# Ten blocks of GpSimd's key parts made in the matrix memory layer instead of the expert layer

## The reference

```
x = x + _L0_xattn_ref(_layernorm(x), ctx_2048, mask)       # one-head attention over the context
x = x + _L0_attn_ref(_layernorm(x), ...)                   # matrix memory (mLSTM), 8 heads, then a gated MLP
x = x + _L0_ffn_ref(_layernorm(x), ...)                    # 16 experts, top 2, and a shared part
x = x + _L1_xattn_ref(_layernorm(x), ctx_2048, ctx_2048)   # 16-head causal attention over the context
```

```
def _rmsnorm(x, w): return w * x * rsqrt(mean(x * x) + 1e-6)
h = _mlstm_parallel(q, k, v, i_pre, f_pre)                 # scores times exp(D - max), by head, causal
h_norm = h * rsqrt(mean(h * h, over the head's 32) + 1e-6) * mh_w
x1 = x + (sigmoid(o_pre) * h_norm) @ w_out
```

## Time and profile before

| | us |
|---|---|
| median of 3 runs | 1100.19 (1099.86 to 1101.62) |
| the profiled execution | 1103.23 |
| its span, first to last instruction | 1101.4 |
| TensorE busy | 1041.8 (95%) |
| VectorE busy | 698.0 (63%) |
| ScalarE busy | 504.3 (46%) |
| GpSimd busy | 234.0 (21%) |

### The profile page before, as it was taken

How to read it: one execution, slowest core, us unless ns; L and a number is a source line. 1 busy time by engine, 2 the same in 40 slices (tenths; PEclk the granted TensorE clock), 3 DMA queues, 4 the chain that set the end, 5 groups by cost and what they waited for, 6 DMA issues and landing times.

```text
span 1101.4 us, 23433 instructions
## 1 busy us (share of the span) xinstructions
PE 1041.8 (95%) x9611; PEld 845.6 (77%) x9611; DVE 698.0 (63%) x1330; ACT 504.3 (46%) x876; POOL 234.0 (21%) x360
## 2 busy tenths in 40 slices
PE   8999999998999989999988899999999999999886
PEld 3765778875777646677775788999999999999764
DVE  3655243247788368888744876776666577677466
ACT  3242232126677448888855624433342233332384
POOL 4701048402132000000010711110001043332120
PEclk9999999999999999999999999999999999999997
DMA  9712346554673517000141000131111122100000
GB/s 383 299 69 79 133 164 214 191 148 121 184 193 106 178 41 263 2 2 2 40 153 40 1 1 20 33 120 41 39 39 58 40 77 68 59 20 10 1 1 10
DMA packets 37158, 100.39 MB, mean 91 GB/s; under 512 B 4033, under 2 KB 12609, under 8 KB 35393
## 3 DMA queue, kind: packets, MB, share of 16 engines
q1 hardware_dynamic: 33152, 87.35, 24.2%
q0 software_dynamic: 2752, 9.44, 2.5%
q10 hardware_dynamic: 1152, 2.16, 0.5%
HBM read 83.73 MB, written 15.20 MB: 90 GB/s over the span
## 4 chain that ended last, share of the span: by engine, by line
PE 81%; DVE 12%; ACT 3%; issue 2%; DMA 1%; POOL 1%; SPq 0%; DVEq 0%; ACTq 0%; POOLq 0%
PE ps L2276 11%; PE ps L2233 10%; PE ps L422 8%; PE ps L1434 6%; PE ps L1790 6%; PE ps L2131 4%; PE ps L2120 4%; PE ps L480 3%; PE ps L1781 3%; PE ps L1582 3%; PE ps L1593 3%; PE ps L415 3%; PE ps L1097 2%; PE ps L1089 2%; PE ps L291 1%
## 5 line engine op out<-in xcount | busy, mean ns | idle before, releaser
L2276 PE MATMUL ps<-vv,prob 128*128 128x129 f32 x1024 | 126.5, 276 | 1.7 <-DVE xn L2463 1.7
L2276 PEld LDWEIGHTS ps<-vv,prob 128*128 128x128 f32 x1024 | 119.6, 191 | 2.5 <-ACT prob L2382 2.1
L2415 DVE TENSOR_REDUCE probT<-ps 128x128 f32<-128x1024 f32 x64 | 82.5, 1290 | 21.9 <-PE ps L2233 12.9
L1716 DVE TENSOR_REDUCE st<-ps 128x1 f32<-128x512 f32 x128 | 82.4, 686 | 18.0 <-PE ps L1582 16.0
L2382 ACT ACTIVATE prob<-prob 128x1024 f32<-128x1024 f32 x64 | 71.1, 1111 | 27.4 <-DVE prob L2427 27.4
L2355 ACT COPY w<-ps 128x128 f32<-128x128 f32 x32 | 8.5, 266 | 160.0 <-PE ps L2242 160.0
L422 PE MATMUL ps<-xT,big 128*128 128x256 f32 x352 | 79.8, 381 | 0.7 <-ACT xT L707 0.7
L2427 DVE TENSOR_TENSOR prob<-ps,probT 128x1024 f32<-128x1024 f32 x64 | 79.6, 1285 | 1.1
L1663 ACT ACTIVATE prob<-ps 128x1024 f32<-128x1024 f32 x64 | 65.8, 1030 | 28.0 <-PE ps L1593 26.8
L422 PEld LDWEIGHTS ps<-xT,big 128*128 128x128 f32 x352 | 66.2, 190 | 11.2 <-ACT xT L707 0.9
L152 POOL TENSOR_SCALAR small<-small 128x4 f32<-128x4 f32 (+1 forms) x44 | 9.9, 226 | 300.3 <-DVE small L2170 156.3
(11 more groups left out here) (476 smaller groups left out, 2282.6 us busy)
## 6 DMA issues: line engine op xcount, KB each, us to landing
big<-blocks_in SPq DMA_DIRECT2D x22, 768.0 KB, 4.3
big<-ctxT_in SPq DMA_DIRECT2D x24, 512.0 KB, 4.1
key_parts<-w POOLq DMA_DIRECT2D x16, 384.0 KB, 4.7
kt<-key_parts SPq DMA_DIRECT2D x32, 192.0 KB, 3.3
vv<-ctx_in SPq DMA_DIRECT2D x2, 2176.0 KB, 24.9
vv<-early_values SPq DMA_DIRECT2D x4, 1088.0 KB, 12.0
kt<-ctxT_in SPq DMA_DIRECT2D x2, 2048.0 KB, 12.4
kt<-key_parts SPq DMA_DIRECT2D x32, 128.0 KB, 3.2
```

What stands on the lines that cost most here:

```text
L1716: dve.tensor_reduce(self.mx[:, u % 2, n:n + 1], k.ps[:, n % 2, :], AX.X, ALU.max).then_inc(s("reduced"), 1)
L2276: last = pe.matmul(k.ps[:, 7, 0:DH + 1], self.prob(u)[:, ch * P:ch * P + P], v, start=(ch == 0), stop=(ch == MC))
L2415: dve.tensor_reduce(self.largest[:, h * P:(h + 1) * P], bank.rearrange("p (c t) -> p t c", t=P), AX.X, ALU.max).then_inc(s("c3_max"), 1)
```

## The change

`Mlstm.gpsimd` gets the range of its roots as arguments. GpSimd makes nine of its last ten blocks (6 to 14) between the first root and the second, and the last (15) between the second and the third. The wait for the fifth gated block goes. The rest of the list keeps its order, so norm 2 is followed at once by the memsets of `n1.gpsimd`. What each instruction computes is unchanged.

```diff
     @staticmethod
-    def gpsimd(k, pool, o):
+    def gpsimd(k, pool, o, first, last):
         s = k.s
-        for n in range(3):
+        for n in range(first, last):
             pool.wait_ge(s("sum_squares"), n + 1)
...
     BLOCKS = [(i, b, c) for b in range(B) for c in range(DC) for i in range(4)]
-    BEFORE_MLSTM = 6
+    BEFORE_MLSTM, LAST = 6, 15
...
             Norm.gpsimd(k, pool, o, 1)
-            Mlstm.gpsimd(k, pool, o)
+            Mlstm.gpsimd(k, pool, o, 0, 1)
+            split.gpsimd(pool, o, split.BEFORE_MLSTM, split.LAST)
+            Mlstm.gpsimd(k, pool, o, 1, 2)
+            split.gpsimd(pool, o, split.LAST, len(split.BLOCKS))
+            Mlstm.gpsimd(k, pool, o, 2, 3)
             Norm.gpsimd(k, pool, o, 2)
-            pool.wait_ge(s("block_h"), 5)
-            split.gpsimd(pool, o, split.BEFORE_MLSTM, len(split.BLOCKS))
             n1.gpsimd(pool, o)
```

## The result

| | before | changed |
|---|---|---|
| median of 5 runs | 1100.19 us | 1110.11 us (1109.16 to 1115.2) |
| the profiled execution, and its span | 1103.23, 1101.4 | 1112.58, 1110.7 |

The ratio is 1.0098, 95% interval 1.0073 to 1.0123. A second set of runs of the same kernel beside the last experiments gave 1.0095 (1.0073 to 1.0117). So the change costs 9.9 us in the medians where 3.4 were forecast. The way was right, but the forecast was a third of the size, and the time is outside the range. Executions in the chip's slower state (one of e5, two of the kernel before beside e5 to e8) are left out of every mean and ratio.

The account below looks back on a forecast made before the run. VectorE's chain was taken to bound the matrix memory partly, TensorE the expert stretch. Waits of 4.24 less 0.78 gave +3.4, rounded down, so median 1100.19 becomes 1103.6, range 1101.2 to 1105.6.

Parts of the forecast that it names:

- The alternation in the matrix memory: Around the second root, VectorE and GpSimd take turns; VectorE's waits reaching the path add 4.24 us.
- the expert rounds' 0.78: Expert stretch: with ten blocks gone, five slowed rounds return to 5.18 each, gaining 0.78 us.
- the rule: VectorE operations with two SBUF inputs, or fast ones, wait for GpSimd's operation in flight; PSUM-input operations and reductions don't.
- The small-operations rival: Matrix memory: L622, L632 and L633 don't wait, other waits stay; net +1.7, 1101.9; chance 0.10.
- The other side: Matrix memory: VectorE's waits are covered by TensorE's early pieces, or only GpSimd waits; 1099.4; chance 0.08.
- GpSimd in time for the roots: Matrix memory: nine blocks end at 103.1, second root wanted at 106.6; tenth at about 115, third wanted at 118.6.
- The late-blocks rival: Between first and second root, transfers delay each block by 1 more; net +8.9, 1109.1; chance 0.05.
- The moved memset: GpSimd's 3.51 memset moves to about 143.5 beside the router's small VectorE operations; 0 to 0.3 each way, taken as 0.
- The clock: TensorE's clock drops in new idle gaps, matmuls at 1.2 GHz add 2.5; net +5.9, 1106.1; chance 0.02.
- the gap ahead of L762: Matrix memory: longest new TensorE idle gap, put at about 2.1, considered for a clock drop.

Follow-up runs that it names:

- e5: Changed kernel with the wait for the fifth gated block back before the memsets and the tenth block behind the third root; ratio 1.0033.
- e8: Kernel before with blocks 6 to 8 between the first and second root, seven left in the expert layer; ratio 0.9996.
- e1: Changed kernel with the wait for the fifth gated block back before the causal layer's memsets; median 1107.68, ratio 1.0055.
- e6: Kernel before with blocks 6 to 10 between the third root and norm 2, blocks 11 to 15 in the expert layer; ratio 1.0002.
- e2: Kernel before with only the two memsets moved right behind norm 2, the ten blocks left in the expert layer; median 1108.24, ratio 1.0063.
- e7: Kernel before with 40 extra GpSimd memsets of 128x1024 between the first and second root; ratio 0.9986.
- e10: Changed kernel with TensorE's idle time ahead of norm 2 filled by 14 small identity matmuls; ratio to before 1.0059.
- e11: Changed kernel with the same TensorE idle time filled by 4 dense f32 products; ratio to before 1.0066.
- e4: Changed kernel with the 3x4096 memset cut into eight of 3x512; median 1107.94, ratio 1.0079.

## Why the prediction was wrong

**The alternation in the matrix memory (forecast 4.24): the mechanism was right, and the size by some luck.** The profiled execution gives 5.3 there. About 0.6 of that (an estimate) is a fall of the clock at 106 to 110, which isn't in the forecast: L1089's 16 matmuls took 3.37 for 1.85, and TensorE's early pieces ended at 115.15 where VectorE's L649 was done at 114.52. At full clock e1 has +3.6 with the expert rounds' 0.78 won, against the forecast of 3.46. The single waits: L622 0.83 and 0.83 (forecast 0.30 and 0.85), L600 0.36 (0.92), L641 0.35 (0.56), second L632 0.79 (0.84), L647 to L649 1.45 in all (1.58). L632's and L633's first waits were 0.11 and 0 (forecast 0.15 and 0.48). L595's and L616's waits (0.97 and 0.39) were not in the sum at all, and L581's was 1.23 where 0.3 had been left out as covered. So the rule was right, the single collisions were off by up to 1.0, and the sum came out because what was missed and what was put too high cancelled. The small-operations rival fell: L622 waited in full. The other side, by which hardly any wait reaches the path, fell too: L762's first product started 2.2 later than before, once the 0.6 ahead of the change is taken off.

**GpSimd in time for the roots: right.** The ninth block was out at 103.8 and the second root was wanted at 107.4. The late-blocks rival fell.

**The expert rounds' gain of 0.78: right** in the changed kernel's chain. What e6's expectation read into it, that only the later blocks do harm, fell with e6.

**The moved memset (forecast 0 to 0.3, taken as 0): the step that failed.** The prediction named the memset's new place, but put only the router's small operations beside it. It doesn't name L193, which starts in the very microsecond that GpSimd becomes free, since both wait for the same root. L193 took 3.73 for 0.41, and e2 shows 3.8 ± 0.9 for the memset by itself. The prediction had the rule (a fast operation waits for the GpSimd operation in flight) and didn't apply it here. L193 can be taken for a slow operation, with 0.41 for 256 elements where the fast L600 takes 0.29. But its like with an input in PSUM shows what it is:

```profile
49.74 0.54 DVE L387 TENSOR_SCALAR att<-ps,st 128x256 f32<-128x256 f32 x1
```

Same shape, two scalars from a tile as well, 0.54 with the input in PSUM and 0.41 in SBUF. PSUM by itself doesn't cost that: L640 with an input in PSUM and L641 without take 0.42 each for 256 elements. VectorE's two-input operations take 0.69 for 512 elements (L648) and 1.22 for 1024 (L621), 1.04 ns an element, so 256 elements at twice that speed save 0.13, which is the difference. By this estimate L193 is a fast operation with a longer start, and a fast one waits even for a GpSimd instruction that only writes, as L600 does in e7.

**The clock (rival with chance 0.02, priced at 2.5): real, and 4.4 ± 0.6.** It was weighed for the gap ahead of L762, which was 0.84 (0.86 in the second batch) and not 2.1, and dismissed by a stretch with 1.5 of idle time in 5, of which 1.37 was one gap. The gap that counted was the one that the memset made, 3.16 in one piece: 3.0 in the profiled execution, and with it filled (e10, e11) the mean loss is 5.0 and 4.3 instead of 8.7. A loss of 3.4 ± 1.1 comes without the memset's gap, as e1's 7.1 against before's 3.7 shows. What causes that one stays open, and so does how the two add up.

In sum: 3.6 at full clock as forecast for the blocks, 2.4 more for the memset behind them (3.3 in the trace, 3.8 alone, errors of 0.5 in the first and 0.9 in the last), and 4.4 by the clock. The forecast had the first of the three.

## What to carry to other kernels

When work moves on one engine, look at everything behind it in that queue and not only at what is moved. Taking a wait away lets the next instruction start at once, and the first to look at is what another engine starts at that same event: L193 in the change, L661 in e5 and e6. A long GpSimd instruction that only writes, even one over three partitions, belongs where VectorE has no fast operation from SBUF. In e7 those with two SBUF inputs or an input in PSUM went on beside it unchanged. And to tell whether a VectorE operation is one that GpSimd can hold, compare its time with the same shape from PSUM. Here that rests on one pair, L193 and L387.

## What the hardware showed

- The run-to-run spread of this kernel is mostly TensorE's clock. Over 19 runs of the kernel before the spans go from 1096 to 1105 with a standard deviation of 2.5, and their product with the mean clock has one of 1.1. Outside the stretches of this change the profiled executions fall to 1.2 GHz at a few places (12 to 16, 272 to 286, 396 to 404, from 1082 on), in some executions and not in others. Where looked at, TensorE had just been idle: busy 0.55 of 2 at 270 to 272 before the fall at 272.
- A memset of GpSimd over 3 partitions held a VectorE operation over 128 partitions for 3.3, and forty memsets over 128 partitions did nothing to VectorE's operations with two SBUF inputs (e7). Cut into eight pieces, the same memset held it for 0.3 at each of two operations (e4).
- A stretch at 1.2 GHz cost 3.0 behind one idle time of 3.16: the loss by the clock can be as large as the wait ahead of it.
